# Cross attention's weighted sum turned round: padded values stationary, probabilities moving, with a new order of the turn and of the start

## The reference

```python
scores = jnp.einsum('bhqd,bhkd->bhqk', q, k) / jnp.sqrt(jnp.float32(hd))      # hd = 8, 16 heads
scores = ALPHA * (scores * mask) + (1.0 - ALPHA) * scores
scores = jnp.clip(scores, -SCORES_CLAMP, SCORES_CLAMP)
attn = jax.nn.softmax(scores, axis=-1)
context = jnp.einsum('bhqk,bhkd->bhqd', attn, v)
out = context.transpose(0, 2, 1, 3).reshape(B, Qlen, D) @ Wo + bo
resid = query + out                                                           # then layer norm
```

## Time and profile before

| | |
|---|---|
| median of 3 runs | 1531.11 us (1527.61 to 1534.62) |
| the profiled execution | 1535.24 us |
| its span, first to last instruction | 1533.5 us |
| PE busy (matmul) | 1452.1 us, 95% |
| PE weight loads | 1266.2 us, 83% |
| DVE, ACT, POOL busy | 1077.5, 743.7, 819.2 us |
| granted TensorE clock, mean | 0.989 |

### The profile page before, as it was taken

One profiled execution on the slowest core, in us unless ns is written; L12 is line 12 of the kernel. 1 busy time (PEld: TensorE's weight loads), 2 busy tenths in 40 slices (PEclk: granted clock), 3 DMA queues, 4 the chain that ended last, 5 costly groups with the idle time before them and its releaser, 6 DMA issues.

```text
span 1533.5 us, 56339 instructions
## 1 busy us (share of the span) xinstructions
PE 1452.1 (95%) x21795; PEld 1266.2 (83%) x21795; DVE 1077.5 (70%) x3025; ACT 743.7 (49%) x1869; POOL 819.2 (53%) x1169
## 2 busy tenths in 40 slices
PE   1589999999999999999999999999999999999997
PEld 1478888888888888888888888888888888888886
DVE  3257777777777777777777777777777777777763
ACT  1125545555554545555454555545455554545543
POOL 2135655655565565556556555655655565565553
PEclk9979999999999999999999999999999999999998
DMA  7122232232232222223222322322232232223210
GB/s 204 27 87 81 96 95 77 83 98 83 80 97 95 75 86 97 84 78 99 95 72 89 97 84 77 100 95 70 91 97 83 76 102 92 70 93 97 83 50 34
DMA packets 159394, 133.15 MB, mean 87 GB/s; under 512 B 69558, under 2 KB 141771, under 8 KB 159243
## 3 DMA queue, kind: packets, MB, share of 16 engines
q1 hardware_dynamic: 159370, 132.83, 27.7%
HBM read 41.04 MB, written 24.61 MB: 43 GB/s over the span
## 4 chain that ended last, share of the span: by engine, by line
PE 92%; SPq 3%; DMA 2%; DVE 1%; issue 1%; ACT 1%; POOL 0%; POOLq 0%; ACTq 0%; DVEq 0%
PE psum L907 16%; PE psum L942 10%; PE psum L919 9%; PE psum L955 9%; PE psum L977 8%; PE psum L969 6%; PE psum L912 4%; PE psum L948 4%; PE psum L962 4%; PE psum L1086 4%; PE psum L933 2%; PE psum L900 2%; PE psum L901 2%; PE psum L902 2%; PE psum L1001 2%; PE psum L926 2%
## 5 line engine op out<-in xcount | busy, mean ns | idle before, releaser
L551 POOL TENSOR_TENSOR ug<-tanh_gate,half_gate 128x384 f32<-128x384 f32 x64 | 64.0, 1001 | 512.7 <-ACT half_gate L600 512.7
L907 PE MATMUL psum<-xnT,wqkv 128*128 128x128 f32 x2048 | 275.3, 283 | 0.1
L907 PEld LDWEIGHTS psum<-xnT,wqkv 128*128 128x128 f32 x2048 | 249.2, 195 | 4.5 <-ACT xnT L560 0.2
L609 ACT ACTIVATE probs<-psum 81x512 f32<-81x512 f32 x256 | 145.4, 593 | 142.1 <-PE psum L948 142.0
L560 ACT ACTIVATE vall<-psum 64x512 f32<-64x512 f32 x256 | 152.1, 594 | 123.3 <-PE psum L902 118.6
L723 DVE TENSOR_TENSOR ra<-psum,rope 128x512 f32<-128x512 f32 x256 | 174.6, 682 | 29.6 <-PE psum L907 29.6
L728 DVE TENSOR_TENSOR z<-psum,wT 77x512 f32<-77x512 f32 x256 | 163.7, 679 | 42.3 <-PE psum L912 42.3
L494 POOL TENSOR_SCALAR z<-z 77x512 f32<-77x512 f32 x256 | 156.0, 623 | 43.4 <-DVE z L728 43.4
L942 PE MATMUL psum<-qT,kall 64*81 64x64 f32 x4096 | 177.1, 237 | 0.0
L723 DVE TENSOR_TENSOR rb<-psum,rope 128x512 f32<-128x512 f32 x256 | 174.3, 681 | 0.0
L919 PEld LDWEIGHTS psum<-v,z 77*64 77x64 f32 x4096 | 134.5, 142 | 44.1 <-issue 36.6
(11 more groups left out here) (134 smaller groups left out, 2599.4 us busy)
## 6 DMA issues: line engine op xcount, KB each, us to landing
rs<-rb SPq DMA_DIRECT2D x256, 256.0 KB, 2.4
q_stack<-q_dram SPq DMA_DIRECT2D x256, 48.0 KB
seq_in<-in SPq DMA_DIRECT2D x64, 166.5 KB
q_dram<-q_parts SPq DMA_DIRECT2D x64, 128.0 KB, 1.9
k_stack<-k_dram SPq DMA_DIRECT2D x64, 115.5 KB
k_dram<-k_parts SPq DMA_DIRECT2D x64, 77.0 KB, 2.1
q_dram<-q_parts SPq DMA_DIRECT2D x64, 64.0 KB, 1.7
out<-out_sb SPq DMA_DIRECT2D x64, 64.0 KB, 1.6
```

The lines of the kernel that those rows point to most:

```text
L907: last = mm(at(name)[:, S * n:S * (n + 1)], wqkv[:, lo + 128 * n:lo + 128 * (n + 1)], xnT[:])
```

## The change

**On PE.** The operands of the cross-weighted sum change places. `v0` is padded from 9 to 32 columns per head (8 values, one column of ones, 23 zeros set once) and is stationary; the head's `z0` (77 keys x 128 queries) moves. The four heads of a group write to partitions 0, 32, 64 and 96 of bank `u`, that is to the four column groups of the array. All 16 heads stand in one block now. The result has values on partitions, so ACT copies the bank (`u`, 128 x 512) to SBUF, and PE turns it in four transposes into bank `pv`, which DVE divides as before (by a wider access, 32 columns a head).

**The order.** Every engine's turn is written in another order, the banks are dealt anew, and the pipeline's cut moves (maxima of heads 8 to 15 are now the first work of PE's turn, both value projections come late in the turn before). ACT's exponentials and masks of groups 2 and 3 are taken in the other order.

**The start.** All contexts are loaded right behind the first inputs. Four loads (`c_tables`, `to_mem_tokens_w`, `to_qkv_w`, the learned keys) are issued by ACT in the first turn, and the other weights by SP behind the second sequence's inputs. The memory tokens are computed in turn -3, behind the output projection.

```diff
-        v0 = sb("v0", [S2, H, VROW])
+        v0 = sb("v0", [S2, H, 32])
+        u = sb("u", [128, GROUP * S])
...
+            ("u", 4, 3, (u_kept,)),
...
+        early_loads = [(stage2[:], c_tables), (wmem[:], to_mem_tokens_w), (wqkv[:], to_qkv_w),
+                       (pm_sb[:].rearrange("n (h d) -> n h d", h=H), persist_mem.rearrange("h n d -> n h d"))]
...
                     if first(seq[4]):
-                        sp.dma_start(wqkv[:], to_qkv_w).then_inc(wqkv_in, 16)
+                        context_loads()
+                if first(seq[3]):
+                    other_weights()
...
-            for t in (*vall, half_gate, tanh_gate):
+            for t in (*vall, half_gate, tanh_gate, v0):
...
+                    act.wait_ge(u_filled, done[4])
+                    copy(u[:], at("u")).then_inc(u_kept, 1)
...
+                    if first(seq[4]):
+                        first_weights()
...
             def weigh_cross(g):
                 for r in range(GROUP):
-                    for s in range(NSEG):
-                        h, tokens = GROUP * g + r, slice(SEG * s, SEG * (s + 1))
-                        last = mm(at("pv")[tokens, VROW * h:VROW * (h + 1)], z0[:, h, tokens], v0[:, h, :])
+                    head = GROUP * g + r
+                    last = mm(at("u")[32 * r:32 * (r + 1), S * g:S * (g + 1)], v0[:, head, :], z0[:, head, :])
...
+                    free(pe, "u", n, 3)
+                    pe.wait_ge(z1_exp, done[4])
+                    weigh_cross(0)
+                    weigh_cross(1)
+                    pe.wait_ge(z2_exp, done[4])
+                    weigh_cross(2)
+                    weigh_cross(3).then_inc(u_filled, 1)
+                    if first(seq[3]):
+                        pooled_tokens()
...
+                    pe.wait_ge(u_kept, done[4])
+                    for g in range(GROUP):
+                        last = nc.tensor.transpose(at("pv")[:, S * g:S * (g + 1)], u[:, S * g:S * (g + 1)], ident[:])
+                    last.then_inc(pv_filled, 1)
```

More of the change, by code:

```diff
@@ L540, in body @@
                 if seq[1] is not None:
-                    pool.wait_ge(ms1_ready, done[2])
+                    wait(pool, x1_ready, done[1])
+                    passed(pool, pool_passed)
+                    nc.gpsimd.tensor_scalar(y_keep[:], y[:], 1.0, 0.0, ALU.mult, ALU.add).then_inc(ykeep_ready, 1)
+                if seq[2] is not None:
+                    pool.wait_ge(var0_ready, done[3])
+                    nc.gpsimd.tensor_tensor(st0[:, 3:4], st0[:, 2:3], nhalf[:], ALU.pow).then_inc(rstd0_ready, 1)
@@ L566, in _, with first_weights @@
             act.wait_ge(zeros_set, 4)
+            def first_weights():
+                for dst, src in early_loads:
+                    act.dma_start(dst, src).then_inc(early_in, 16)
             def gate_biases():
@@ new lines, in body @@
+                if seq[1] is not None:
+                    dve.wait_ge(out_filled, done[2])
+                    dve.wait_ge(ykeep_ready, done[2])
+                    V.tensor_tensor(x1[:], at("out")[:, 0:D], y_keep[:], ALU.add).then_inc(x1_ready, 1)
+                if seq[3] is not None:
+                    dve.wait_ge(mean_ready, done[4])
+                    V.tensor_scalar(st0[:, 2:3], st0[:, 1:2], LN_EPS, None, ALU.add).then_inc(var0_ready, 1)
+                    V.scalar_tensor_tensor(out=t0g[:], in0=r0[:], scalar=st0[:, 0:1], in1=ga_rep[:], op0=ALU.subtract, op1=ALU.mult).then_inc(centred_ready, 1)
@@ new lines, in body @@
+                if seq[2] is not None:
+                    dve.wait_ge(max01_filled, done[3])
+                    largest(0).then_inc(max0_ready, 1)
+                    largest(1).then_inc(max1_ready, 1)
+                if seq[1] is not None:
+                    dve.wait_ge(x1_ready, done[2])
+                    V.tensor_tensor_reduce(out=x1sq[:], in0=x1[:], in1=x1[:], scale=1.0 / D, scalar=RMS_EPS, op0=ALU.mult, op1=ALU.add,
+                                            accum_out=st1[:, 0:1]).then_inc(ms1_ready, 1)
@@ L863, in _ @@
+                if seq[2] is not None:
+                    dve.wait_ge(max1_ready, done[3])
+                    V.tensor_scalar(mt[:, 0, :], mx[:], -1.0, None, ALU.mult).then_inc(mt_hi_ready, 1)
+                if seq[3] is not None:
+                    dve.wait_ge(rstd0_ready, done[4])
+                    dve.wait_ge(centred_ready, done[4])
+                    V.scalar_tensor_tensor(out=y[:], in0=t0g[:], scalar=st0[:, 3:4], in1=be_rep[:], op0=ALU.mult, op1=ALU.add).then_inc(y_ready, 1)
             pipeline(dve, body)
@@ L1087, in body @@
                     last.then_inc(down_filled, 1)
+                if seq[3] is not None:
+                    free(pe, "wo", n, 3)
+                    pe.wait_ge(c0T_ready, done[4])
+                    mm(at("wo")[:, 0:D], c0T[:], wo[:]).then_inc(wo_filled, 1)
+                    if first(seq[3]):
+                        memory_tokens()
                 if seq[4] is not None:
```

463 lines of the change are left out of this document (212 added, 251 removed).

## The result

| | before | after |
|---|---|---|
| median | 1532.84 us (4 runs) | 1453.5 us (4 runs, 1450.09 to 1455.0) |
| the profiled execution, its span | 1535.24, 1533.5 us | 1452.16, 1450.2 us |
| granted clock, mean | 0.989 | 0.992 |

The ratio is 0.9485, with a 95% interval of 0.9453 to 0.9516. The forecast was 1500 us with a range of 1472 to 1540: the sign was right, and the gain of 79 us more than twice the 31 forecast.

A forecast was written before the change was run, and what follows sets the result against it. PE's work bounds the 22.38 us turn, tied with the stacks chain between `k1` and cross scores. 1535.24 - 9 (60 turns of 22.2) - 20 (start) - 3 (end) = 1503; as a median 1499, say 1500 us, range 1472 to 1540.

The forecast's parts named there:

- k to x: From first `k1` projection to first cross scores: stays 10.74 us by the stacks chain; PE's work there some 10.25.
- x to s: From first cross scores to the transpose of `mt`: 9.2 us a turn, against 9.80 before.
- s to k: From the transpose of `mt` to the first `k1` projection: 2.28 us a turn, against 1.84 before.
- The block: PE's new weighted sum, 32 records over four column groups at once: 1.0 us, upper end 1.84, against 2.07 before.
- The stacks chain: `k1`, `q1`, rotary products, swaps, `k_stack`, four `q_stack` issues: still 10.74 us, PE newly waiting about 0.5 at first cross scores.
- The tie between `mt` and PE: Ahead of the transpose of `mt`: DVE's chain 2.67, 2.96 us from L977's end, against 2.95 of PE work.
- The end: Draining turns make no stacks, so the wait at the cross scores goes and PE's saving counts: -3 us.
- The start: Earlier second-sequence inputs (-10 us) and moved memory tokens (-10 to -12, less 1 to 2): -20, between nothing and -30.
- Rival 1: Column groups only pair or moving reads collide: block 1.84 us, turn 23.05, total 1549, slower; chance 0.13.
- Rival 2: Stacks chain has unseen slack, so the turn is PE's 21.75 us: total 1470; chance 0.14.
- Rival 3: Other chains (`mt`, `z2_exp`) tighter: 0.2 to 0.3 us more, turn 22.4, total 1518; chance 0.23 together with Rival 4.
- Rival 4: The start gives nothing because the loads collide: total 1520 us; chance 0.23 together with Rival 3.

The follow-up runs named there:

- experiment 1: Kernel after the change with one of the four `q_stack` DMA issues left out: 1423.19 us, ratio 0.9272, turn 20.85 us.
- experiment 2: Kernel before the change with one of the four `q_stack` DMA issues left out: 1522.79 us, ratio 0.9919, turn 22.26 us.
- experiment 3: Kernel before, with only L977 moved from the head of PE's turn to the end of the turn before: 1513.68 us, ratio 0.9871.
- experiment 8: Kernel after, with the input projection put between the halves of the new weighted-sum block: 1496.93 us, ratio 0.9753.
- experiment 7: Three variants of kernel after: two heads of a column group in a row, 1453.83 us; extra block in one group, 1681.5; extra block in four groups, 1508.59.
- experiment 4: Kernel after, with the old weighted sum of 64 records, no copy and no transposes: 1552.66 us, ratio 1.0112.
- experiment 6: Kernel before, with the new sum in two half blocks at the old places, the copy and the transposes: 1535.55 us, ratio 1.0012.
- experiment 5: Kernel after with the old weighted sum, its second half moved behind the turn of the maxima and the input projection: 1580.0 us, ratio 1.0304.

## Why the prediction was wrong, step by step

**The failed step** is the sentence "PE's own work falls to 22.38 - 2.07 + 1.0 + 0.44 = 21.75 us a turn". It carried over all of PE's turn outside the weighted sum unchanged. By experiments 1 and 2, PE's own work was 22.26 and became 20.85: 1.41 less, not 0.63. From the starts of PE's records, medians of 39 turns:

| | us a turn | forecast |
|---|---|---|
| weighted sum: -2.075 + 0.987 + 0.442 | -0.65 | -0.63 |
| branch hidden behind L922 (experiment 3) | -0.31 | 0 |
| passages from one kind of matmul to another | -0.45 | 0 |

The third is many small terms, each the time of a line's last record to the next start. A matmul over the full array takes 0.11 before one of its own kind and 0.20 before one in row or column groups (L1003 ahead of L1007 before, L1036 ahead of L967 after: the input projection is 0.82 us in the earlier trace rows and 0.73 after, 620.22 to 620.95). The transposes of `xnT` and `hnT` fell from 0.26 and 0.17 to 0.12 and 0.11 when the L919 block that stood between them left; L1110 takes 0.14 of its own where L1050 took 0.32. Against these, L1004 takes 1.98 where L977 took 1.78; small bf16 matmuls follow it now, L900 with 512 columns moving before. That the branch costs 0.31 is shown by an experiment; the passages are read from the traces, and only experiment 8 made one on purpose (0.09).

**Where it went in the parts.** For k to x the working did allow 0.27 for fewer passages, and got PE's work there right (10.25; measured 10.21), in part by luck: it started from 10.74, in which 0.15 was the hidden wait of experiment 2, and the passages gave 0.16. But x to s was then found by subtraction from 21.75, so that what k to x had saved was added to x to s: "21.75 - 2.28 - 10.25 = 9.2". Summed from its own rows, x to s is 9.80 less the input projection 0.82, less one old block 1.04, plus the new block 1.0: 8.94; without the branch 8.63, which is what was measured, since the passages of this part cancel (L1004's 0.20 more against about the same saved in smaller ones). For s to k the same holds: 2.28 forecast, 1.99 measured, the difference being 0.09 in the projection and 0.20 in the two transposes. With these two numbers the forecast would have been 1.99 + 10.74 + 8.63 = 21.36 a turn, and its own sum 1451 us for the profiled execution, where 1452.16 was measured.

**What held.** The block at 1.0 (0.99). The stacks chain at 10.74 (10.68), with a new wait of about 0.5 at *x* (0.45). The tie between `mt` and PE ahead of *s* (2.67 forecast, 2.70 measured, a wait of some 0.1). The end at -3 (-2.1). The start at -20 (-18.1) held as a sum, and that was luck: the second projection came 4.2 us earlier and not 10, and the other 13.9 were gained behind it, where 10 to 12 less 1 to 2 had been put. The first stacks were late by 9.4 us; ACT's loads took 3.8 of it, within the 3 to 5 that the prediction called thinkable, but the contexts took 5.6 where it had 2.

**The rivals.** Rival 1 (groups pair only) is out: experiment 7. Rival 2 named 21.75 a turn and no wait; the turn was below that although there is a wait, so it came near the time for a reason that was not its own. Rival 3 (other chains tighter) cost 0.1 at `mt`. It becomes real where cover is moved, as experiments 4, 6 and 8 show with waits of 0.38, 0.49 and 0.46. Rival 4 (nothing from the start) is out. The range ended at 1472, just inside the 1470 of rival 2, which rested on the same 21.75: a bound that shares the forecast's error is no bound.

**Open.** What tips the granted clock in experiments 4 and 5. And the passages, 0.45 us a turn: they are read from the records of two kernels that differ in much else, and no run changes them one by one.

## What to carry to other kernels

When a change rewrites the order, sum PE's work in each part of the turn from the starts of its records, passage by passage and with the branch as a row of its own, instead of subtracting the changed operation from the turn and handing the remainder to one part. Look for what each new operation must cover or be covered by: here the swap alone gave nothing, the new order and start without it lost 1%, and all together gave 5%. Once a chain on a DMA queue binds, what stands ahead of it in that queue is the next thing to move.

## What the runs showed of the hardware

- Four column groups, each with 32 columns stationary and 128 float32 columns moving, run at the full factor of four: 0.027 us a record against 0.110 in one group. Two heads of one group in a row cost less than 0.1 us a block.
- With the same 64 records of 9 columns the granted clock holds in one order (0.989 over the run); in two others it falls behind the last of them, to 0.61 over 4.4 us, in 19 or 29 of 45 turns, 1.2 us each time. What tips it is not shown.
- A loop's branch costs PE 0.31 us behind 0.28 us of small matmuls, and nothing that shows behind a matmul with 512 columns moving (0.33 to the next start with it and without).
- The same small DMA store landed after 2.3 us with no large loads ahead of it, after 6.2 behind four loads issued by ACT, and after 11.9 behind these and SP's eight context loads.
